# A Mamba and mixture-of-experts kernel: decays in PSUM, the scan in two halves, fifteen of sixteen drives on GpSimd, one F bank and one K bank

## The reference

```python
# patches of 64 images -> 37 tokens each (36 patches and a class token), 256 wide
out = jnp.concatenate([cls, proj], axis=1) + pos_enc
# mixer: D_INNER 512, 16 states, a causal convolution of 4 taps
x_d = _silu(conv(x_d) + conv_b)
ssm_in = jnp.einsum('btd,kd->btk', x_d, W_x)          # dt (1), B (16), C (16)
delta = jax.nn.softplus(dt_raw * W_dt[:, 0] + b_dt)
dA = jnp.exp(d_t[..., None] * A)                      # decay
h = dA * h + d_t[..., None] * b_t[:, None, :] * u_t[..., None]
y = jnp.einsum('bds,bs->bd', h, c_t)
y = (y + D_param * x_d) * _silu(z)
h1 = layernorm(x + y @ W_out.T)
# router: 32 experts in 8 groups, 4 groups, 8 experts a token; then the experts
out = out + w[:, None] * ((silu(flat @ wg.T) * (flat @ wu.T)) @ wd.T)   # and a shared expert
```

## Time and profile before

| what | us |
|---|---|
| median of 3 runs | 1308.86 (1306.77 to 1310.47) |
| the profiled execution | 1309.32 |
| its span | 1307.5 |
| DVE busy | 1082.3 (83%) |
| PE busy | 1043.1 (80%) |
| POOL busy | 664.6 (51%) |
| ACT busy | 608.4 (47%) |
| period of a tile in the mixer stage | 82.7 |

### The profile page before, as it was taken

How to read it: one execution, slowest core, us unless ns; L and a number is a source line. 1 busy time by engine, 2 the same in 40 slices (tenths; PEclk the granted TensorE clock), 3 DMA queues, 4 the chain that set the end, 5 groups by cost and what they waited for, 6 DMA issues and landing times.

```text
span 1307.5 us, 16414 instructions
## 1 busy us (share of the span) xinstructions
PE 1043.1 (80%) x4783; PEld 793.6 (61%) x4783; DVE 1082.3 (83%) x1866; ACT 608.4 (47%) x1530; POOL 664.6 (51%) x801
## 2 busy tenths in 40 slices
PE   4778879788797887978879778676529999999980
PEld 4666657456574665756657556344318888888860
DVE  6689899899999999989989999999414467777773
ACT  1564444434545345453453544533006666666650
POOL 6000183561854818547075382773740067776675
PEclk7999889899898988988989989888759999999995
DMA  4598010020110201102011010014735679898882
GB/s 156 187 372 292 5 49 18 7 84 1 52 40 7 80 5 51 40 7 84 1 43 49 7 50 15 15 56 184 272 106 168 176 230 275 259 280 257 266 260 82
DMA packets 104361, 150.05 MB, mean 115 GB/s; under 512 B 13968, under 2 KB 91216, under 8 KB 103889
## 3 DMA queue, kind: packets, MB, share of 16 engines
q1 hardware_dynamic: 87377, 107.20, 25.2%
q0 software_dynamic: 16896, 41.80, 11.1%
HBM read 72.12 MB, written 76.82 MB: 114 GB/s over the span
## 4 chain that ended last, share of the span: by engine, by line
PE 38%; DVE 31%; issue 20%; POOL 4%; DMA 3%; SPq 1%; ACT 1%; DVEq 0%; POOLq 0%; ACTq 0%
PE BC L907 10%; DVE arena L1209 10%; PE Y L757 6%; DVE arena L1201 5%; PE K L919 5%; DVE arena L1217 5%; PE F L692 4%; PE Y L901 3%; PE K L769 2%; DMA mixer_own<-pool_dram 2%; PE F L705 2%; POOL pool_dram L602 2%; PE F L708 1%; PE F L913 1%; POOL gat L631 1%
## 5 line engine op out<-in xcount | busy, mean ns | idle before, releaser
L1209 DVE TENSOR_TENSOR_SCAN arena<-arena 128x888 f32<-128x888 f32 (+1 forms) x176 | 342.9, 1948 | 0.3
L757 PE MATMUL Y<-arena,ident 128*128 128x444 f32 (+1 forms) x704 | 328.0, 597 | 4.5 <-DVE arena L1217 4.5
L602 POOL DMA_INDIRECT pool_dram<-hrow,slot_of x176 | 241.3, 1371 | 60.6 <-issue 52.7
L631 POOL DMA_INDIRECT gat<-y_dram,slot_all x176 | 176.6, 1003 | 144.8 <-DMA y_dram<-mixer_own 87.9
L983 ACT ACTIVATE arena<-mixer_own,aneg 128x216 f32<-128x216 f32 (+1 forms) x384 | 145.5, 453 | 188.5 <-DVE arena L1209 142.4
L983 ACT ACTIVATE arena<-arena,aneg 128x216 f32<-128x216 f32 x320 | 124.7, 464 | 169.0 <-DVE arena L1209 128.6
L739 PE MATMUL BC<-bc_rows,sel 96*128 96x222 bf16 (+1 forms) x352 | 66.5, 273 | 157.8 <-DVE arena L1217 157.7
L757 PEld LDWEIGHTS Y<-arena,ident 128*128 128x128 f32 x704 | 135.3, 212 | 83.9 <-issue 74.5
L907 PE MATMUL BC<-arena,xt 128*128 x716 | 185.4, 382 | 0.0
L1217 DVE TENSOR_TENSOR arena<-arena,BC 128x888 f32<-128x888 f32 (+1 forms) x176 | 183.5, 1042 | 0.0
L535 POOL TENSOR_TENSOR seen<-seen,count 128x32 f32<-128x32 f32 x10 | 16.5, 1649 | 270.6 <-ACT count L1027 270.6
(11 more groups left out here) (214 smaller groups left out, 1603.7 us busy)
## 6 DMA issues: line engine op xcount, KB each, us to landing
mixer_own<-pool_dram SPq DMA_DIRECT2D x179, 144.0 KB, 3.7
y_dram<-mixer_own SPq DMA_DIRECT2D x179, 128.0 KB
pool_dram<-filler SPq DMA_DIRECT2D x5, 4176.0 KB, 29.5
arena<-in_experts_dram SPq DMA_DIRECT2D x1, 7680.0 KB, 21.3
arena<-in_x_dram SPq DMA_DIRECT2D x10, 648.0 KB, 4.2
pool_dram<-filler SPq DMA_DIRECT2D x1, 4896.0 KB, 32.2
arena<-in_experts_dram SPq DMA_DIRECT2D x1, 4608.0 KB
pool_dram<-hrow,slot_of POOLq DMA_INDIRECT x176, 2.8
```

Of the source, the lines that this page charges most:

```text
L602: nc.gpsimd.indirect_dma_start(out=pool_rows, out_offset=bass.IndirectOffsetOnAxis(ap=slot_of[q][0:r, b, k:k + 1], axis=0), in_=hrow[q][0: ...
L631: nc.gpsimd.indirect_dma_start(out=gat[0:r, k, b, :], out_offset=None, in_=y_rows[0:blocks_by(t) * P, :], in_offset=bass.IndirectOffsetOnA ...
L757: mm = nc.tensor.matmul(Y[j][:, 0:w], ident[:], read[g % 3][:, j * w:(j + 1) * w], start=False, stop=(s == STATES - 1), skip_group_check=True)
L1209: nc.vector.tensor_tensor_scan(state[g % 2][:, 0:w], decay[g % 3][:, 0:w], drive[g % 2][:, 0:w], 0.0, ALU.mult, ALU.add).then_inc(scan_don ...
```

## The change

- The decays go into two PSUM banks D[0], D[1], one for each half of the channels; there is one buffer for each half. `decays(g + 1, b)` waits for the scan of half b of state g. The scan is issued as two instructions of half the width.
- The drives of states 1 to 15 are formed on POOL from a copy of row B in SBUF that ACT makes (`copy_b`, one of four buffers), two states ahead; there are four drive buffers. The drive of state 0 stays on DVE (`drive_first`). `spread(g)` writes C of state g and B of state g + 1.
- F and K are one bank each. The convolution's third chunk waits for SiLU of the first two; dt is in F, B and C are in K beside the parts of tile t; z is projected in two halves, one after the other. The waits between these users are new or other than before.
- POOL's order is by state: scatters of tile i - 2 one or two a state in states 1 to 10, the refinement in state 5, allocation in three parts in 12 to 14, the series product in 13, closing in 15.
- ACT and PE pieces stand at other states, and ACT loads its function tables after the softplus logarithm and at state 15.

```diff
-        decay = [carve(KI * N) for _ in range(3)]
         at_drive = taken[0]
-        drive = [carve(KI * N) for _ in range(2)]
+        drive = [carve(KI * N) for _ in range(DRIVES)]
         state = [carve(KI * N) for _ in range(2)]
         read = [carve(KI * N) for _ in range(3)]
-        assert taken[0] == ARENA
+        b_row = [carve(N) for _ in range(B_ROWS)]
...
-        F = [ps("F0"), ps("F1")]
-        K = [ps("K0"), ps("K1")]
-        PX, PG, PH, PY = Y, BC, F, K
+        D = [ps("D0"), ps("D1")]
+        F = ps("F")
+        K = ps("K")
+        PX, PG, PH, PY = Y, BC, D, [F, K]
...
+            def drives(g):
+
+                i = g // STATES
+                pool.wait_ge(b_copied, pooled(g + 1))
+                if g % STATES == 1:
+                    pool.wait_ge(du_done, i + 1)
+                if g >= DRIVES:
+                    pool.wait_ge(scan_done, 2 * (g - DRIVES + 1))
+                nc.gpsimd.tensor_tensor(cut(drive[g % DRIVES], i), cut(du[i % 2], i),
+                                        b_row[g % B_ROWS][:, None, 0:width(i)].broadcast_to([P, KI, width(i)]), ALU.mult
+                                        ).then_inc(drive_done, 1)
...
+                if i >= 2 and mix and 1 <= s <= 10:
+                    for at in range(8 * (s - 1) // 5, 8 * s // 5):
+                        scatter(i - 2, at // TOPK, at % TOPK)
+                if back and s == 5:
+                    refine_mixed(t)
+                if back and mix and s in (12, 13, 14):
+                    if s == 12:
+                        allocating[0] = allocation(t)
+                    next(allocating[0])
+                if front and s == 13:
+                    multiply_series(n)
+                if back and mix and s == 15:
+                    close(t)
                     if i == TILES - 1:
                         prepare_last()
-                if i + 1 < TILES:
-                    multiply_series(i + 1)
-                if i >= 1:
...
+            for i in range(-1, TILES):
+                for s in range(STATES):
+                    g = STATES * i + s
+                    if 0 <= g + 2 < STATES * TILES and (g + 2) % STATES > 0:
+                        drives(g + 2)
+                    pieces(i, s)
+            for at in range(2 * TOPK):
+                if at == TOPK:
+                    refine_mixed(TILES - 1)
+                scatter(TILES - 2, at // TOPK, at % TOPK)
+            for at in range(2 * TOPK):
+                scatter(TILES - 1, at // TOPK, at % TOPK)
...
-                if c == 2 and k == 0 and n > 0:
-                    pe.wait_ge(bc_split, SPLITS * n)
+                if c == 2 and k == 0:
+                    pe.wait_ge(x2_done, 2 * n + 1)
...
             def project_z(i, b):
-                if i > 0:
-                    if b == 0:
-                        pe.wait_ge(base_done, i)
+                if b == 1:
+                    pe.wait_ge(z2_done, 2 * i + 1)
+                else:
+                    if i > 0:
+                        pe.wait_ge(rank_taken, i)
                     else:
-                        pe.wait_ge(rank_taken, i)
-                else:
-                    pe.wait_ge(mixer_in, 16 * len(MIXER_LOADS))
+                        pe.wait_ge(mixer_in, 16 * len(MIXER_LOADS))
+                    if i + 1 < TILES:
+                        pe.wait_ge(bc_split, SPLITS * (i + 1) + 2)
...
+                if (g + 1) % STATES == 0 and g + 1 < STATES * TILES:
+                    pe.wait_ge(bc_split, SPLITS * ((g + 1) // STATES + 1))
+                    if g < 0:
                         pe.wait_ge(sel_step, 4)
+                if g == 1:
+                    pe.wait_ge(first_drive, 1)
                 if g >= 2:
                     pe.wait_ge(read_done, g - 1)
-                w = width(i)
-                for j in range(2):
-                    mm = nc.tensor.matmul(BC[g % 2][:, j * w:(j + 1) * w], sel[:, STATES * j + s, :], bc_rows[i % 2][:, 0:w],
-                                          start=True, stop=True)
+                for j, state_ in ((0, g + 1), (1, g)):
+                    if 0 <= state_ < STATES * TILES:
+                        i, s = divmod(state_, STATES)
+                        w = width(i)
+                        mm = nc.tensor.matmul(BC[g % 2][:, j * N:j * N + w], sel[:, STATES * j + s, :], bc_rows[i % 2][:, 0:w],
+                                              start=True, stop=True)
                 mm.then_inc(bc_done, 1)
...
-                pe.wait_ge(ex_done, t + 1)
+                if t < TILES - 1:
+                    pe.wait_ge(base_done, t + 1)
...
+                if mix and s == 1:
+                    start_y(i)
+                if back and s in (2, 3):
+                    project_out(t, s - 2)
+                if front and s in (4, 5):
+                    convolve(n, 2, s - 4)
+                if back and s == 6:
+                    turn_h1(t)
                 if back and s == 7:
                     route(t)
+                if front and s in (6, 7):
+                    convolve(n, 3, s - 6)
+                if back and s == 8:
                     shared_gate_up(t)
-                if front and s == 8:
-                    convolve(n, 3, 0)
...
+                    project_dt(n)
+                if back and mix and s == 10:
                     shared_down(t)
...
+                if back and s == 11:
+                    rank_chosen(t)
...
+                if front and s == 11:
+                    project_bc(n)
+                if mix and s in (12, 14):
+                    project_z(i, (s - 12) // 2)
+                if i + 2 < TILES and s in (12, 13):
+                    project_patches(i + 2, s - 12)
...
-            def decays(g):
+            def copy_b(g):
+
+                w = width(g // STATES)
+                act.wait_ge(bc_done, g + 1)
+                if pooled(g) >= B_ROWS - 1:
+                    act.wait_ge(drive_done, pooled(max(g - B_ROWS + 1, 0)))
+                nc.scalar.activation(b_row[g % B_ROWS][:, 0:w], BC[(g - 1) % 2][:, 0:w], ACT.Copy).then_inc(b_copied, 1)
+
+            def decays(g, b):
                 i, s = divmod(g, STATES)
-                if g >= 3:
-                    act.wait_ge(scan_done, g - 2)
-                elif g == 0:
+                if g >= 1:
+                    act.wait_ge(scan_done, 2 * (g - 1) + b + 1)
+                elif b == 0:
                     act.wait_ge(mixer_setup, 1)
-                if s == 0:
...
+                for c in range(2):
                     last = nc.scalar.activation(
-                        decay[g % 3][:, c * w:(c + 1) * w].rearrange("p (a t) -> p a t", t=TOKENS)[:, :, 1:TOKENS],
-                        cut(delta[i % 2], i)[:, c, :].rearrange("p (a t) -> p a t", t=TOKENS)[:, :, 1:TOKENS],
-                        ACT.Exp, scale=aneg[:, s, c:c + 1])
+                        D[b][:, c * w:(c + 1) * w].rearrange("p (a t) -> p a t", t=TOKENS)[:, :, 1:TOKENS],
+                        cut(delta[i % 2], i)[:, 2 * b + c, :].rearrange("p (a t) -> p a t", t=TOKENS)[:, :, 1:TOKENS],
+                        ACT.Exp, scale=aneg[:, s, 2 * b + c:2 * b + c + 1])
                 last.then_inc(decay_done, 1)
...
                 act.wait_ge(rank_done, t + 1)
+                if t + 2 < TILES:
+                    act.wait_ge(rows_done, t + 3)
...
+                if front and s == 3:
+                    tanh_conv(n, 0)
+                if back and s == 6:
+                    normalise(t)
+                    copy_h1t(t)
+                if back and s == 7:
+                    logit_exp(t)
+                if front and s == 8:
+                    tanh_conv(n, 1)
+                if back and s == 9:
+                    shared_gate(t)
+                if front and s in (10, 11):
+                    take_dt(n, 2 * (s - 10))
+                    take_dt(n, 2 * (s - 10) + 1)
+                if back and mix and s == 11:
+                    take_ranks(t)
+                if front and s == 11:
+                    softplus_exp(n)
...
+                    if mix:
+                        tanh_gate(i, 0)
...
+                if mix and s == 15:
+                    tanh_gate(i, 1)
...
-                    if 0 <= g + 2 < STATES * TILES:
-                        decays(g + 2)
+                    for b in range(2):
+                        if 0 <= g + 1 < STATES * TILES:
+                            decays(g + 1, b)
+                    if 0 <= g + 2 < STATES * TILES and (g + 2) % STATES > 0:
+                        copy_b(g + 2)
...
+                rows, bank = bc_rows[n % 2], K[:, N:2 * N]
                 dve.wait_ge(rows_done, n + 1)
+                if n > 1:
+                    dve.wait_ge(rank_taken, n - 1)
...
-            def drives(g):
+            def drive_first(i):
+                dve.wait_ge(bc_done, STATES * i + 1)
+                dve.wait_ge(du_done, i + 1)
```

(45 more changed lines are left out.)

279 lines of the change are left out of this document (99 added, 180 removed).

## The result

The changed kernel takes 1335.56 us (median of four runs, 1334.90 to 1340.47) against 1308.99 for the kernel before beside it: ratio 1.020, 95% interval 1.0177 to 1.0223. It is slower, by 26.6 us; 1340 was forecast. The profiled execution spans 1333.2 us.

The account below looks back on a forecast made before the run. DVE was taken to bound the mixer; afterwards DVE, POOL and PE have floors of 65 to 68 us, and waits make a tile 86 against 82.7. With +30 or 31 us on 1309.3, 1340 us was forecast, range 1313 to 1365.

Parts of the forecast that it names:

- The walk of a tile: Following one full mixer tile through the engines' queues: losses of 18.5 on a floor of 68, 86 us taken against 82.7.
- scan of state 8: DVE, ready at 31.5, waits for ACT's decays, which stand behind the normalise and POOL's refinement, until 35.6: 4.1 us lost.
- The product: POOL's series product, queued behind drive(15) and two thirds of the allocation, ends at 79.8 and delays DVE's softplus: 2.0 lost.
- the floor of 68: DVE's work in a tile: sixteen steps 49.6 us, one drive and 17.5 of pieces, 68 us.
- The floor of 68 a tile: POOL's work in a tile: drives 32 us, scatters 20, allocation and closing 12.5, refinement 1.6, product 2.1; 68, from 48.
- Both early signs of being wrong: On POOL: a drive taking clearly less than 2 us, or gaps before the refinement, would first show the forecast wrong.
- PSUM as source at no cost: Reading decays from PSUM in DVE's scans adds 0; upper bound 0.06 us a half, 2 us a tile.
- The sum: Whole kernel: eight tiles +26, last tile +6, first tile -4, before it +2; together +30 or 31 us, giving 1340.
- The reason given for the lost slack: In the mixer: slack is gone through one decay buffer per half for three, and one F and one K bank for two.
- the floors rule: Rival: the three engines overlap nearly fully, 71 to 76 us a tile, 1190 to 1262 us in all; chance 0.17.
- the fast rival: Rival of nearly full overlap, 1190 to 1262 us, chance 0.17; decides if POOL's refinement is through by about 27 us.
- Locking: DVE and POOL instructions with two SBUF inputs exclude each other; without scans from PSUM fifteen drives each lose up to 2 us.

Follow-up runs that it names:

- Refinement first: Changed kernel with POOL's refinement ahead of state 5's two scatters instead of behind them; ratio 0.9943 to the kernel before, 82.0 us a tile.
- Drives on DVE: Changed kernel with all sixteen drives back on DVE and ACT's copies of B gone; ratio 0.9909 to the kernel before, 81.8 us a tile.
- router ahead: The "ranks first" kernel with drives of states 0 to 2 on DVE and the router ahead of the second SiLU; ratio 0.9594 to the kernel before.
- the repeat: The changed kernel measured again, unchanged; ratio 1.0225 to the kernel before, 30.8 us slower, 86.9 us a tile.
- ranks first: Changed kernel with scatters moved out of states 4 and 5, product ahead of allocation, ACT's rank copy before the last dt channels; ratio 0.9677 to before.
- scatters apart: Changed kernel with scatters two each in states 1, 2, 3 and 6 to 10, none in 4 and 5; ratio 0.9928 to the kernel before.

## Why the prediction was right, and where it was not

- **The walk of a tile** gave 86.8 and 86 was taken; 86.1 was measured. Its losses by place, forecast and measured: scan of state 8 4.1 and 3.8; second SiLU 4.3 and 4.0; split 2.15 and 2.0; product 2.0 and 3.1; gate tanh 0.6 and 0.5; states 9 and 10 1.2 and 0.5; moments (from 18.5 and a SiLU of 0.6 to 21.0) 1.9 and 1.1. These are of a tile of 85.2 us. The refinement was to end at 32.5 and did at 31.8. "Refinement first" shows that this place, not the sum of loads, sets the tile. That the total of the walk came out so close is in part luck: the waits sum to 15.0 where it had 18.5, and DVE's own time is 71.1 where it had 68.
- **The product** is the term that was under-sized: the walk put it behind drive(15) and two thirds of the allocation and had it end 2.0 late, it was 3.1.
- **DVE**: halves 1.06 and a step of 3.07 for 1.09 and 3.1; a drive 1.91 for 2.06, which moved nothing. DVE's own time was 71.1, 3 over the floor of 68, of which 2.1 are slot_of and the router's first row, blocked; the walk had 1 of blocking in the router.
- **POOL's busy time** was to be some 75 of 90 us and was 64.2. The floor of 68 a tile counted scatters from start to start; they are busy 0.96 of 1.25. Both early signs of being wrong showed a little, a drive of 1.91 and gaps of 0.82 to 1.57 ahead of the refinement, and yet it came when the walk said: drive(5) starts at 17.6 us of the tile for 17.9, drive(6) at 21.5 for 21.8, drive(7) at 25.8 for 26.4.
- **PSUM as source at no cost**: right for the scan. Halves of 296 columns took at least 744 ns from PSUM and 742 from SBUF. The 2.1 us a tile by the Trainium skill (VectorE: DVE Perf Modes, the TRN2 errata) did not appear; the measurement decides.
- **The sum**: eight tiles +28.0 for +26; last tile and end +6.1 for +6; before the first +1.9 for +2; the first tile -6.7 for -4; the tile before the scatters -3.6 for 0. The last two are the sizes that failed: the walk was made for a full tile only, and without scatters or back part DVE's shorter step shows through. They took 6.3 of the 30 and 2.0 came back on the eight.
- **The reason given for the lost slack was wrong.** The prediction put it down to one decay buffer per half in place of three and to one F bank and one K bank, and held that against the floors rule. "Drives on DVE" has the same buffers and banks and runs at 81.8; "router ahead" has them with thirteen drives on POOL and runs at 76.6. So the 3.5 us a tile against before do not come from them but from the order, in which the refinement stands behind drives and scatters. What more buffers would give on top was not tried.
- **The point at which the fast rival decides was not reached.** It was put at a refinement through by 27 us. No run with drives on POOL had it before 28.2, not even with all scatters behind it. At 29.6 the tile is already 82.0; four changes of place and two drives reached 76.6, just over the 71 to 76 of that rival.
- **Locking**: that without the decays in PSUM each drive would lose up to 2 us was right in kind (10.7 a tile) and wrong in who pays: DVE's scans.

## What to carry to other kernels

When work moves to a third engine, walk its queue with the instructions that others wait for, and put the short one that starts a chain (here four small instructions of 1.6 us) ahead of bulk work: two swapped lines were worth 35 us, more than the whole change cost. A wait in the profile is not its own price. The 3.1 us for the product were worth 1.2 to 2.5 a tile in one order and 3.4 in another, 1.3 us off the split's wait were worth nothing, and 2.4 us less waiting on TensorE brought 1.8 more behind it. Before two orders are compared by a mean, look at single tiles: here the same kernel has tiles of 85.2 and of 88.9 us, by how long TensorE takes to restart. And look for the idle time in a stretch before it is called gapless.

## What the runs showed of the hardware

- Scans with both inputs in SBUF on DVE and drives on POOL hold each other up, and here DVE paid most: half scans 1.06 to 1.49 us on the mean, drives 1.91 to 2.12. POOL's indirect DMA instructions rose too, from 0.96 to 1.23:

```profile
L616 POOL DMA_INDIRECT pool_dram<-hrow,slot_of x176 | 215.7, 1226 | 47.2 <-issue 39.9 <-DVE slot_of L1448 5.0 <-DVE arena L1278 1.7
```

- Behind a wait of 3.72 us TensorE lost 1.8 more in its next three rows (add-up 2.67 for 1.67), behind one of 1.35 nothing. In "refinement first" that is nearly half of what the edit gave. Behind the same wait of 3.7 it lost 1.0 to 1.2 more again in some tiles of the same kernel (two of eight, four of eight in the repeat).
- The same expert stage took 291 to 297 us for some kernels and 411 to 416 for others, with the mixer's length the same within 2 us by the sum above. It is not shown that the chip makes the difference: "ranks first" (297) and "router ahead" (416) bear the same chip number. In the short one TensorE is busy 249 of 250 us at a granted clock of 1.00 (changed kernel, 1020 to 1270), in the long one 281 of 350 us at 0.85 ("scatters apart", 1000 to 1350), with less moved by DMA (172 GB/s for 244). What makes it wait stays open.
